# A macaron block on one core: the near bias of the heads' maxima as a bf16 product, query tiles packed in nine banks a head

## What is computed

```python
def _L1_attn_ref(x, Wq, Wk, Wv, Wo, rel, ln_gamma, ln_beta):
    ...
    scores = jnp.einsum('bhid,bhjd->bhij', q, k)
    i = jnp.arange(T)
    dist = jnp.clip(i[:, None] - i[None, :], 0, MAX_REL)
    bias = rel[:, dist]
    scores = scores + bias[None]
    causal = i[:, None] >= i[None, :]
    scores = jnp.where(causal[None, None], scores, -jnp.inf)
    attn = jax.nn.softmax(scores, axis=-1)
    y = jnp.einsum('bhij,bhjd->bhid', attn, v)
    ...
```

## Time and profile before

| | us |
|---|---|
| median of 3 runs | 2555.85 |
| the 3 runs | 2555.43, 2555.85, 2562.52 |
| span of the profiled execution | 2554.8 |
| TensorE busy | 2128.9 (83%) |
| VectorE busy | 1539.1 (60%) |
| ScalarE busy | 970.2 (38%) |
| chain that ended last, by engine | PE 61%, DVE 26%, ACT 5% |
| granted TensorE clock, mean | 0.903 of full |

### The profile page before, as it was taken

How to read it: one execution, slowest core, us unless ns; L and a number is a source line. 1 busy time by engine, 2 the same in 40 slices (tenths; PEclk the granted TensorE clock), 3 DMA queues, 4 the chain that set the end, 5 groups by cost and what they waited for, 6 DMA issues and landing times.

```text
span 2554.8 us, 38679 instructions
## 1 busy us (share of the span) xinstructions
PE 2128.9 (83%) x12842; PEld 1592.0 (62%) x12842; DVE 1539.1 (60%) x4444; ACT 970.2 (38%) x1961; POOL 314.8 (12%) x298
## 2 busy tenths in 40 slices
PE   4589999957999956899999456578998998999846
PEld 2478888856788935788888335434445545555435
DVE  7744343446455577434343598576876776778287
ACT  4122232322333342232323334235556556555532
POOL 4320000031000044100000432311002002000000
PEclk8699999978999978999999657579999999999956
DMA  8110111020000031110110310422422422422001
GB/s 260 43 64 24 31 30 31 26 64 26 1 1 1 1 116 58 51 31 27 29 30 26 91 44 25 73 46 58 51 28 51 74 29 54 72 29 27 2 25 50
DMA packets 84036, 114.84 MB, mean 45 GB/s; under 512 B 12212, under 2 KB 73816, under 8 KB 80728
## 3 DMA queue, kind: packets, MB, share of 16 engines
q1 hardware_dynamic: 77416, 94.80, 17.0%
q0 software_dynamic: 6432, 17.57, 2.2%
HBM read 69.16 MB, written 43.17 MB: 44 GB/s over the span
## 4 chain that ended last, share of the span: by engine, by line
PE 61%; DVE 26%; ACT 5%; issue 4%; DMA 2%; POOL 2%; DVEq 0%; ACTq 0%; SPq 0%; POOLq 0%
PE psum L775 10%; PE psum L777 10%; PE psum L776 10%; PE psum L126 5%; PE psum L2298 4%; PE psum L128 4%; PE psum L127 4%; DVE mt L2186 3%; PE psum L2277 3%; PE psum L862 3%; DVE m L2174 2%; PE psum L2257 2%; DVE stats L160 2%; DVE m L2183 2%; DVE xn L185 2%
## 5 line engine op out<-in xcount | busy, mean ns | idle before, releaser
L2137 ACT ACTIVATE pt<-psum 128x512 f32<-128x512 f32 (+3 forms) x768 | 333.9, 492 | 274.9 <-DVE psum L2212 180.1
L740 DVE SCALAR_TENSOR_TENSOR h<-psum,xg,sg 128x128 f32<-128x128 f32 x592 | 166.7, 344 | 415.6 <-PE psum L862 415.6
L556 ACT ACTIVATE sg<-psum 128x512 f32<-128x512 f32 x180 | 107.7, 598 | 575.1 <-PE psum L777 575.1
L775 PE MATMUL psum<-w_hi,xt_hi 128*128 (+1 forms) x720 | 285.6, 397 | 33.7 <-DVE xt_lo L705 33.7
L776 PE MATMUL psum<-w_lo,xt_hi 128*128 (+1 forms) x720 | 283.8, 394 | 0.0
L777 PE MATMUL psum<-w_hi,xt_lo 128*128 (+1 forms) x720 | 283.7, 394 | 0.0
L2257 PE MATMUL psum<-ks,qs 96*128 96x512 bf16 (+3 forms) x768 | 235.5, 347 | 36.0 <-DVE m L2174 10.2
L2277 PE MATMUL psum<-qs,ks 99*128 99x512 bf16 (+3 forms) x768 | 239.0, 334 | 24.4 <-ACT pt L2137 18.8
L775 PE MATMUL psum<-w_hi,ht_hi 128*128 (+1 forms) x720 | 218.1, 303 | 0.2
L2186 DVE CUSTOM_DVE_ANT_0 mt<-psum,band_q 128x256 bf16<-128x256 f32 (+1 forms) x512 | 204.2, 399 | 18.3 <-PE psum L2257 8.1
L2281 PE MATMUL psum<-band,ident_r 128*128 128x256 f32 (+1 forms) x864 | 214.8, 337 | 0.0
(11 more groups left out here) (284 smaller groups left out, 4420.1 us busy)
## 6 DMA issues: line engine op xcount, KB each, us to landing
xg<-w_dram SPq DMA_DIRECT2D x54, 256.0 KB, 3.2
qk_scr<-parts SPq DMA_DIRECT2D x32, 384.0 KB, 2.5
qs<-qk_scr SPq DMA_DIRECT2D x96, 128.0 KB, 7.2
ks<-qk_scr SPq DMA_DIRECT2D x96, 128.0 KB, 7.8
xg<-rows_in SPq DMA_DIRECT2D x74, 132.0 KB, 2.1
rows_out<-yb SPq DMA_DIRECT2D x74, 128.0 KB, 1.7
x<-x_dram SPq DMA_DIRECT2D x4, 1024.0 KB, 8.6
out_dram<-x SPq DMA_DIRECT2D x4, 1024.0 KB, 4.5
```

Of the source, the lines that this page charges most:

```text
L740: ins = dve.scalar_tensor_tensor(out=h[i % 2][:, e, :], in0=u[:, e, :], scalar=xg[j % XSLOT][:, at:at + 1], in1=sg[i % 2][:, e, :], op0=AL ...
L775: pe.matmul(out, a[0], b[0], start=first, stop=False)
L2137: act.activation(pt[n % NPT][:, 0:q1 - q0], st_bank(n)[:, 0:q1 - q0], ACT.Exp).then_inc(*exped.up())
```

## The change

Each query tile's row of keys is now cut in pieces that fill nine banks of 512 columns a head exactly (`PACKS`: 12 pieces, as many as before; the triple is tile, first key, last key; then the width of the groups that are reduced apart, and where their maxima go). A piece that ends at the row's end gets a second product on top of it in the same bank: the bf16 identity `ident_q` by 256 columns (128 for tile 0) of `band_q`, eight a head. VectorE then needs one reduction a bank. The maxima of the parts stand in one tile `m3` (32 columns a head, at the order `ROW_AT`); GpSimd's memset of it is done once, not in every unit, and the row is joined by three reductions instead of one. The stream has 36 + 7 = 43 items a unit. Nothing of the attention proper is changed.

```diff
+                self.ident_q = sb(stack, "ident_q", [P, P], BF16)
...
+                    pool.tensor_copy(self.ident_q[:, :], ident[:, :])
...
+        MS = 4
+        ROW_AT = {0: 0, 6: 1, 2: 2, 4: 3, 1: 4, 3: 5, 5: 6, 7: 7}
+        PACKS = [([(7, 0, 512)], 512, 28, 1), ([(0, 0, 128), (6, 0, 384)], 128, 3, 1),
+                 ([(7, 512, 1024)], 512, 29, 1), ([(6, 384, 896)], 512, 7, 1),
+                 ([(5, 0, 512)], 512, 24, 1), ([(1, 0, 256), (5, 512, 768)], 256, 19, 6),
+                 ([(4, 128, 640)], 512, 13, 1), ([(2, 0, 384), (4, 0, 128)], 128, 9, 1),
+                 ([(3, 0, 512)], 512, 20, 1)]
+        NPACK = len(PACKS)
...
-            per_u = HG * BT + 7
+            per_u = HG * NPACK + 7
...
-                m3 = [sb(st, f"m3{i}", [P, HG * BT, 3]) for i in range(2)]
+                m3 = sb(st, "m3", [P, HG, BT * MS])
...
+                        if kind == "max":
+                            u, h, s = i
+                            pieces, wide, at, step = PACKS[s]
+                            n = BANK // wide
+                            if h == 0 and s == 0:
+                                dve.wait_ge(*(row_max(u) if u else max_zero(1)))
+                            dve.wait_ge(*max_score(nth[i] + 1))
+                            dve.tensor_reduce(m3[:, h, at:at + (n - 1) * step + 1:step],
+                                              mx_ring.bank((kind, i)).rearrange("p (n k) -> p n k", k=wide),
+                                              AXIS.X, ALU.max).then_inc(*part_max.up())
                         elif kind == "max_row":
-                            dve.wait_ge(*near_max((i + 1) * HG * BT))
-                            dve.tensor_reduce(mm[i % 2][:, :], m3[i % 2][:, :, :], AXIS.X, ALU.max,
-                                              negate=True).then_inc(*row_max.up())
+                            dve.wait_ge(*part_max((i + 1) * HG * NPACK))
+                            rows = mm[i % 2][:, :].rearrange("p (h t) -> p h t", t=BT)
+                            parts = m3[:, :, :].rearrange("p h (t k) -> p h t k", k=MS)
+                            for t0, t1, dt in ((0, 7, 6), (2, 5, 2), (1, 8, 2)):
+                                a = ROW_AT[t0]
+                                ins = dve.tensor_reduce(rows[:, :, t0:t1:dt], parts[:, :, a:a + len(range(t0, t1, dt)), :],
+                                                        AXIS.X, ALU.max, negate=True)
+                            ins.then_inc(*row_max.up())
...
+                            o = 0
+                            for t, c0, c1 in PACKS[s][0]:
+                                w = (t + 1) * P
+                                near = c1 == w
+                                ins = pe.matmul(bank[:, o:o + c1 - c0], qs[r][0:KS_ROWS, h, t * P:(t + 1) * P],
+                                                ks[r][0:KS_ROWS, h, c0:c1], start=True, stop=not near)
+                                if near:
+                                    bw = min(w, 2 * P)
+                                    ins = pe.matmul(bank[:, o + w - bw - c0:o + w - c0], tables.ident_q[:, :],
+                                                    band_q[:, u % NHG * HG + h, 2 * P - bw:2 * P],
+                                                    start=False, stop=True)
+                                o += c1 - c0
+                            ins.then_inc(*max_score.up())
```

More of the change, by code:

```diff
@@ L1920, in macaron @@
         LATER = slice(BT, NT)
[L1921 to L1928, removed]
+        MS = 4
+        ROW_AT = {0: 0, 6: 1, 2: 2, 4: 3, 1: 4, 3: 5, 5: 6, 7: 7}
+        PACKS = [([(7, 0, 512)], 512, 28, 1), ([(0, 0, 128), (6, 0, 384)], 128, 3, 1),
[4 rows of a table added]
+        NPACK = len(PACKS)
         def heads_order(project):
             def maxima(u):
-                first = [("max_zero", u)]
                 for h in range(HG):
[L1934 to L1937, removed]
+                    for s in range(NPACK):
+                        yield [("max", (u, h, s))]
                 yield [("max_row", u)]
@@ L2021, in attention_heads @@
             order = heads_order(ahead.steps)
[L2022 to L2026, removed]
+            nth = {i: n for n, i in enumerate(i for kind, i in order if kind == "max")}
+            MX = (*ahead.USES, "max", "max_turn", "y_turn", "yt_turn", "wo")
             mx_ring = Ring([u for u in order if u[0] in MX], [psum[:, 5 + i, :] for i in range(3)])
@@ L2029, in attention_heads @@
             NPT = 3 * HG
-            max_zero, far_ok, far_max, near_ok, near_max, row_max = (S(x) for x in (
-                "max_zero", "far_score", "far_max", "near_score", "near_max", "row_max"))
+            max_zero, max_score, part_max, row_max = (S(x) for x in (
+                "max_zero", "max_score", "part_max", "row_max"))
             max_turned, max_col, max_part = S("max_turned"), S("max_col"), S("max_part")
@@ L2042, in emptied @@
                     return ahead.emptied(use)
-                if kind == "max_far":
-                    return far_max(nth[use] + 1)
                 if kind == "max":
-                    return near_max(nth[use] + 1)
+                    return part_max(nth[i] + 1)
                 s = {"max_turn": max_col, "y_turn": y_div, "yt_turn": yd_ok,
@@ L2064, in attention_heads @@
                 pt = [sb(st, f"pt{i}", [P, BANK if i < 2 * HG else 3 * P]) for i in range(NPT)]
-                m3 = [sb(st, f"m3{i}", [P, HG * BT, 3]) for i in range(2)]
+                m3 = sb(st, "m3", [P, HG, BT * MS])
                 mm = [sb(st, f"mm{i}", [P, HG * BT]) for i in range(2)]
-                mt_all = sb(st, "mt", [P, P])
-                mt, junk = mt_all[0:HG * BT, :], mt_all[:, :].bitcast(BF16)
+                mt = sb(st, "mt", [HG * BT, P])
                 mparts = sb(st, "mparts", [HG * BT, 3, P], BF16)
@@ L2108, in on_pool @@
                         ahead.on_pool(kind, i, mx_ring)
[L2109 to L2113, removed]
+                        if kind == "ones":
+                            pool.memset(m3[:, :, :], LOWEST).then_inc(*max_zero.up())
                             pool.wait_ge(*max_zero(1))
@@ L2167, in on_dve @@
                         ahead.on_dve(kind, i, mx_ring)
[L2168 to L2189, removed]
-                        elif kind == "max_row":
-                            dve.wait_ge(*near_max((i + 1) * HG * BT))
-                            dve.tensor_reduce(mm[i % 2][:, :], m3[i % 2][:, :, :], AXIS.X, ALU.max,
-                                              negate=True).then_inc(*row_max.up())
@@ L2248, in on_pe @@
                         ahead.on_pe(kind, i, clear)
-                        if kind in ("max_far", "max"):
-                            u, h, t = i
-                            w, bw, far, cut = spans(t)
+                        if kind == "max":
+                            u, h, s = i
                             r = u % NR
-                            c0, c1 = (0, cut) if kind == "max_far" else (cut, w)
                             bank = clear((kind, i))
-                            if h == 0 and t == QORDER[0]:
+                            if h == 0 and s == 0:
                                 pe.wait_ge(*stacks_of(r, u))
-                            pe.matmul(bank[:, 0:c1 - c0], qs[r][0:KS_ROWS, h, t * P:(t + 1) * P],
-                                      ks[r][0:KS_ROWS, h, c0:c1], start=True,
-                                      stop=True).then_inc(*(far_ok if kind == "max_far" else near_ok).up())
+                            o = 0
[11 more added lines that the diff above has]
+                            ins.then_inc(*max_score.up())
                         elif kind == "max_turn":
```

## The result

The changed kernel takes 2543.59 us (median of 4 runs, 2542.58 to 2547.16) against 2558.03 us for the kernel before (4 runs): a ratio of 0.9942, with a 95% interval of 0.9924 to 0.9959. It is faster by 14.4 us. I had forecast 2560.7 with a range down to 2545, and gave a time that is faster by more than 0.3% a chance of 0.18.

The account below looks back on a forecast made before the run. TensorE nearly full in the attention, VectorE costing time where TensorE awaits a bank. +51.9 - 43 + 5 - 5 - 3.6 + 0.3 - 1 + 0.3 = +4.9 us, giving 2560.7 us; 8 in 10: 2545 to 2578.

Parts of the forecast that it names:

- Near bias on TensorE: Eight added products a head, 0.865 us, in the 15 units whose maxima run beside attention: +51.9 us (48 to 56).
- VectorE: Maxima cost VectorE 5.40 instead of 5.86 us a head, nine reductions at 0.60; grouped reductions costed like plain ones.
- TensorE's waits for VectorE: TensorE's waits in the attention for VectorE's maxima to free a bank: most go, -43 us (ends 16 and 69.5).
- what comes back: Waits put back because VectorE's in-order queue stands for the projections' first part with maxima behind: +5 us (0 to 22).
- Other waits of TensorE: Longer products between scores hide some waits for the exponential and for a projection's bank: -5 us (0 to -12).
- Unit 0's maxima and the clock: Unit 0's maxima end near 1679 against 1682.53: -3.6 us; denser stream may raise the clock early: -1 us (+2 to -5).
- The stream and the join: Less room with 43 items for 48 steps: +0.3 us once; two more small reductions in unit 0's turn: +0.3 us.
- The signs: Wrong if units without projections (clean units) get shorter, or weight loads still wait for VectorE over 30 us in all.
- projection units within 2 us of before: Expected sign: units with the next batch's projections beside them keep their time within 2 us.
- its 8.3: TensorE's cost a unit for the maxima's existing score products, 4608 columns a head: 8.3 us, 2.1 us a head.
- VectorE's pace: Rival: VectorE sets the pace, added products hide; 2524 us, or 2529 if all 69.5 us of waits go; chance 0.15.
- The rule of the Trainium skill: Judges TensorE's fullness by weight loads: 358 of 722.8 us in the attention, so room for added products; VectorE 514.

Follow-up runs that it names:

- bursts: Nine banks a head with the near bias on VectorE, taken in six items a head, three of which hold two banks: 2535.5 us.
- blanks: Nine banks with the bias on VectorE, plus three extra bank uses a head (product and reduction of 16 columns, result unread): 2561.94 us.
- the two runs with a gap: An empty stream item before the turn of a unit's joined row: in the changed kernel 2546.13 us; in nine banks with bias on VectorE 2530.25 us.

## Why the prediction was wrong

The runs form a square, in us:

| | bias on VectorE | bias on TensorE |
|---|---|---|
| twelve banks a head | 2558.0 (before) | 2564.3 |
| nine banks a head | 2527.3 | 2543.6 (the change) |

- **Near bias on TensorE**: right in the size of its stream, but not in what of it counts. The products stand 0.112 us ahead of the next start for 256 columns (0.115 taken):

```profile
2216.42 0.27 PE L2244 MATMUL psum<-band_q,ident_q 128*128 128x256 bf16 x1
2216.53 0.27 PE L2240 MATMUL psum<-ks,qs 96*128 96x256 bf16 x1
```

  Of the 51.9 us of stream that I forecast, 26.6 count at twelve banks and 35.3 at nine; the prediction took back only what the relief of VectorE gives. My sum of +4.9 us is, by its terms, that of moving the bias alone, and the run that does just this measured +5.5 (its terms were not all tested one by one, so errors in them may cancel).
- **VectorE**: right. A reduction of 512 columns keeps 0.60 us from start to start, and the form in four groups lasts as long (mean 688 ns against 686):

```profile
L2163 DVE TENSOR_REDUCE m<-psum 128x1 f32<-128x512 f32 x384 | 257.6, 686 | 57.0 <-PE psum L2244 39.4 <-PE psum L2240 10.6
...
L2163 DVE TENSOR_REDUCE m<-psum 128x4 f32<-128x512 f32 x128 | 88.0, 688 | 19.2 <-PE psum L2240 17.2
```

- **TensorE's waits for VectorE**: roughly right. Taken as in the prediction (the middle of the two views) and without the turn's own wait they fell from 43 to 7 us, 36 less, against 38 forecast after what comes back.
- **Other waits of TensorE, "-5 us (0 to -12)"**: this is the step that failed. The prediction priced what stands in each bank and never the number of banks. It even wrote that the 12 score products and 4608 columns stay, and passed over that they now take nine turns of the ring instead of twelve. Packing alone is worth 31.6 us with the bias on VectorE (against the runs of before beside it; 30.7 by the table) and 20.7 with it on TensorE. The attention's balance says the same: +51.9 for the products, -36 for the waits on maxima and +9 for the turn would make +25, and -9.4 were measured, so some 34 us of TensorE's time went elsewhere, and not 5. Half of it can be listed. By the products' view TensorE's waits for other things than the maxima, the turn and the first transfer fell from 35.4 to 18.2 us, by 17.2, where my range ended at 12. Those for the exponential went from 18.6 to 14.2, those around the projections and outputs from 16.8 to 4.0. The four largest of these before, then all but two of 0.4 us after:

```profile
PE psum L2257 <- ACT rest L1823: 3.9, 8, 0.6
PE psum L2257 <- DVE rest L1864: 3.8, 11, 0.5
PE psum L126 <- POOL xt_lo L1794: 3.6, 5, 0.9
PE psum L2326 <- ACT rest L2154: 3.1, 6, 0.6
...
PE psum L126 <- POOL xt_lo L1796: 1.9, 2, 1.0
PE psum L2315 <- ACT rest L2142: 1.3, 3, 0.4
```

  Up to 3.9 us more are the clock. The rest was not traced; short waits that the modelled ends cover are one place for it, and a stream that counts for less than 51.9 us another.
- **What a turn of the ring costs.** TensorE can stand at most two uses ahead of the one that is being emptied. A projection's bank is emptied in two steps by ScalarE and VectorE with waits between them. With nine uses a head, more score work lies between a use and its bank's next turn. That is my reading. The runs show that the gain is the packing's (the square), that it falls in the units with projections alone, that two uses in one step take little of it away (bursts), and that uses added back return a part of it (blanks, 10 to 18 of 30.5 us). What makes up the rest stays open; where the stream's steps fall among the projections' moved a single unit by up to 4.1 us in the two runs with a gap, and is one candidate. "Perfetto Trace Analysis" in the Trainium skill, section "Optimization Strategy", says that the same bubble repeating on the engine that should be full can mean too little PSUM for the next tile. With that many short waits for banks in the earlier trace rows the trace agrees that the bubble is there; that more banks would win time, no run here shows.
- **Unit 0's maxima and the clock, -3.6 and -1**: right. The maxima took 3.9 us less; the first score is 5.7 us earlier, 2.0 of them by the earlier start. The clock did rise during the first maxima (mean 0.85), and fell again in the turn, so the first scores ran 5.4 us at half clock, 6.4 before. That the attention also lost two later stretches at half clock, up to 3.4 us of time, was not in the sum.
- **The stream and the join, +0.3 each**: the join was mis-sized. It costs TensorE an idle wait in nearly each unit, 10.8 us in 15 against 1.9 in 5, where I had put it down once. It was not to be had back by a gap.
- **The signs.** Neither of the two by which I would have known myself wrong came up: clean units grew, and weight loads waited for VectorE for 25.8 us in all, under 30. What failed is "projection units within 2 us of before": they lost up to 8.9 us each. Both signs looked at VectorE's maxima, and the error lay where other work shares the banks.
- **A slip.** The maxima's products are 8.6 us a unit at the 0.12 us for 256 columns that the prediction names; its 8.3 is at 0.115. Nothing else hangs on it.
- **The rivals.** VectorE's pace is refuted for the units without projections (unit 11 grew while VectorE's chain share vanished). The rule of the Trainium skill, "Perfetto Trace Analysis", section "Identifying the Most-Contended Engine", on the share of weight loads, by which this rival would have been the forecast, points the wrong way here: loads are busy for 54% of unit 11 after the change (20.8 of 38.8 us) while TensorE has 94% of its chain, and taking the products out again wins 3.0 us there. The time came out on the rival's side for a reason that neither it nor the rule has.

## What to carry to other kernels

Where engines hand buffers round in a small ring, count the uses as well as the work: filling each bank fully was worth 20 to 32 us here, all of it where other work shared the ring; moving the bias from VectorE to TensorE cost 5 to 16. When a diff does two things, price each alone before summing; the best kernel was the half of this change that added no product. When a control lands on the number that you hoped for, look where in the kernel its time falls. And read a chain share as where time passes, not as what a change there can win.

## What was not expected of the hardware

- The same eight products a head cost 26.6 us with twelve bank uses and 35.3 with nine. As I read it, the fewer waits a full engine has left, the closer an added product comes to its full stream (51.9 us forecast).
- A product of 16 columns and a reduction of 16, with a semaphore each way, cost 0.18 us of the kernel's time a pair, twice VectorE's busy time for them (0.09 us) and six times the distance at which TensorE starts its next product when it needn't wait (0.03 us).
